# A gated cross-attention block on Trainium2: SyncE's DMA queue in another order

## The reference

```python
x = x + jnp.tanh(g_xattn[0]) * xattn(ctx, ctx, layernorm(x), mask, Wv, bv, Wk, bk, Wq, bq, Wo, bo)
x = x + jnp.tanh(g_ffn[0]) * jnp.tanh(layernorm(x) @ W1 @ W2 @ W3 + bias)
# xattn: energy = where(mask == 0, min, q @ k.T); softmax(energy / sqrt(16)) @ v, then @ Wo + bo
```

## Time and profile before

| | us |
|---|---|
| median of 3 runs (1081.43 to 1085.96) | 1083.36 |
| the profiled execution | 1079.94 |
| its span | 1078.1 |
| TensorE busy | 1023.4 (95%) |
| VectorE busy | 948.6 (88%) |
| ScalarE busy | 828.6 (77%) |
| GpSimd busy | 806.0 (75%) |

### The profile page before, as it was taken

The page is one execution under the profiler, slowest core; times in us unless marked ns, Lnnn a source line. Parts: engine busy times, 40 slices in busy tenths (PEclk is TensorE's granted clock), DMA queues, the critical chain, the costliest instruction groups (busy, mean ns, idle before and its releaser), DMA issues.

```text
span 1078.1 us, 45335 instructions
## 1 busy us (share of the span) xinstructions
PE 1023.4 (95%) x18487; PEld 892.2 (83%) x18487; DVE 948.6 (88%) x1331; ACT 828.6 (77%) x1275; POOL 806.0 (75%) x1184
## 2 busy tenths in 40 slices
PE   5988999999999999999999999999999999999965
PEld 5777888888888888888888888888888888888855
DVE  5778999998899999989999998899998999999866
ACT  4566888888788888878888788788887887878742
POOL 5245878878788887878888877788787887888753
PEclk9999999999999999999999999999999999999998
DMA  5133555555555555555555556555555555555431
GB/s 154 45 104 106 165 147 161 162 155 152 155 153 164 145 171 155 164 149 149 165 154 162 157 145 173 143 161 159 152 164 150 150 163 149 167 152 154 124 124 69
DMA packets 260400, 158.87 MB, mean 147 GB/s; under 512 B 174945, under 2 KB 227170, under 8 KB 260194
## 3 DMA queue, kind: packets, MB, share of 16 engines
q1 hardware_dynamic: 260050, 155.72, 51.4%
q10 hardware_dynamic: 144, 0.26, 0.1%
HBM read 85.92 MB, written 68.94 MB: 144 GB/s over the span
## 4 chain that ended last, share of the span: by engine, by line
PE 55%; DMA 13%; SPq 13%; issue 7%; POOL 6%; DVE 5%; ACT 1%; POOLq 0%; DVEq 0%; ACTq 0%
PE ps_m L507 11%; PE ps_m L500 11%; PE ps_s L636 9%; PE ps_s L615 8%; PE ps_x L647 7%; PE ps_m L574 5%; DMA scratch_y<-yn 5%; SPq L215 3%; DMA scratch_m<-max_T 3%; PE ps_s L621 3%; SPq L303 2%; SPq L292 2%; DMA q_aug<-scratch_m 2%; PE ps_m L494 2%; DMA den_wide<-scratch_r 2%
## 5 line engine op out<-in xcount | busy, mean ns | idle before, releaser
L1021 DVE TENSOR_TENSOR probs<-ps_s,far_T 128x2048 f32<-128x2048 f32 x128 | 293.3, 2291 | 60.0 <-PE ps_s L636 59.8
L1010 DVE TENSOR_REDUCE neg_max<-ps_s 128x16 f32<-128x2048 f32 x128 | 292.5, 2285 | 26.7 <-PE ps_s L621 26.2
L810 ACT ACTIVATE probs<-probs 128x2048 f32<-128x2048 f32 x128 | 245.0, 1914 | 6.2 <-DVE probs L1021 5.9
L785 ACT ACTIVATE q_aug<-ps_m,q_bias,q_scale 128x256 f32<-128x256 f32 x256 | 123.5, 563 | 58.0 <-PE ps_m L500 48.9
L615 PE MATMUL ps_s<-k_aug,q_aug 32*128 32x128 f32 x4096 | 150.6, 283 | 14.2 <-DVE probs L1021 8.1
L636 PE MATMUL ps_s<-q_aug,k_aug 32*128 32x128 f32 x4096 | 152.1, 283 | 8.5 <-DMA q_aug<-scratch_m 5.8
L615 PEld LDWEIGHTS ps_s<-k_aug,q_aug 32*128 32x128 f32 x4096 | 127.9, 186 | 34.9 <-issue 24.3
L636 PEld LDWEIGHTS ps_s<-q_aug,k_aug 32*128 32x128 f32 x4096 | 127.7, 186 | 27.3 <-DMA q_aug<-scratch_m 9.4
L647 PE MATMUL ps_x<-probs,v_ones 128*32 128x128 f32 x4096 | 139.2, 277 | 3.2 <-issue 2.4
L785 ACT ACTIVATE k_aug<-ps_m,k_bias,parity 128x256 f32<-128x256 f32 x256 | 123.5, 563 | 18.8 <-PE ps_m L500 18.8
L647 PEld LDWEIGHTS ps_x<-probs,v_ones 128*32 128x32 f32 x4096 | 104.7, 110 | 32.7 <-issue 32.6
(11 more groups left out here) (123 smaller groups left out, 1725.9 us busy)
## 6 DMA issues: line engine op xcount, KB each, us to landing
scratch_a<-a_den SPq DMA_DIRECT2D x64, 512.0 KB, 3.7
x_in<-in_x SPq DMA_DIRECT2D x64, 256.0 KB, 4.4
a_rows<-scratch_a SPq DMA_DIRECT2D x64, 256.0 KB
den_wide<-scratch_r SPq DMA_DIRECT2D x64, 256.0 KB
out<-y SPq DMA_DIRECT2D x64, 256.0 KB, 4.7
ctx_in<-in_ctx SPq DMA_DIRECT2D x252, 64.0 KB, 2.7
scratch_y<-yn SPq DMA_DIRECT2D x59, 256.0 KB, 4.3
y_blocks<-scratch_y SPq DMA_DIRECT2D x236, 64.0 KB, 2.4
```

The lines of the kernel that those rows point to most:

```text
L785: last = nc.scalar.activation(dst[:, :, 2 * m + a, :], src[:, m * TOK:(m + 1) * TOK].rearrange("p (n q) -> p n q", q=P), ACT.Identity, bia ...
L810: nc.scalar.activation(tile, tile, ACT.Exp).then_inc(probs_ready, 1)
L1010: nc.vector.tensor_reduce(neg_max[:, 0:H].rearrange("p (j c) -> p j c", j=G), ps_s[:], AX.X, ALU.max, negate=True).then_inc(max_ready, 1)
L1021: nc.vector.tensor_tensor(probs[i % 2][:].rearrange("p j s q -> p (j s) q"), ps_s[:].rearrange("p j s q -> p (j s) q"), far_T[:].unsqueeze ...
```

## The change

Only the order in SyncE's queue changes. Block 0 of the ctx load of pair t + 3 is issued between `read_den` and the even `read_max`, ahead of `write_a` and the x load; blocks 1 to 3 stay where the whole load was. The store, which stood at the head of a pass for pair t - 7, is issued behind `read_a` for pair t - 6. The odd `read_max` is issued ahead of `write_y`. The store of pair NP - 7 that followed the loop falls into it.

```diff
-            def load_ctx(p):
+            def load_ctx_blocks(p, blocks):
                 wait(sp, ctx_turned, p - 1)
-                if p == 0:
-                    sp.dma_start(ctx_in[0][:], ctx_v[:, 0]).then_inc(ctx_landed[0], 16)
-                    return
-                for a in range(G):
+                for a in blocks:
...
             for t in range(NP):
-                if is_pair(t - 7):
-                    store(t - 7)
                 if is_pair(t - 5):
                     read_y(t - 5)
                 write_max(2 * t)
                 if is_pair(t - 2):
                     read_den(t - 2)
+                if is_pair(t + 3):
+                    load_ctx_blocks(t + 3, (0,))
                 read_max(2 * t)
                 if is_pair(t - 2):
                     write_a(t - 2)
                 if is_pair(t + 4):
                     load_x(t + 4)
                 if is_pair(t + 3):
-                    load_ctx(t + 3)
+                    load_ctx_blocks(t + 3, (1, 2, 3))
                 write_max(2 * t + 1)
                 if is_pair(t - 2):
                     write_reciprocals(t - 2)
                     read_a(t - 2)
+                if is_pair(t - 6):
+                    store(t - 6)
+                read_max(2 * t + 1)
                 if is_pair(t - 4) and t - 4 <= END:
                     write_y(t - 4)
-                read_max(2 * t + 1)
                 if is_pair(t - 2):
                     read_wide(t - 2)
             y3, y2, y1, last = NP - 4, NP - 3, NP - 2, NP - 1
-            store(NP - 7)
             read_den(y1)
```

More of the change, by code:

```diff
@@ L217, in load_ctx @@
                                  ).then_inc(ctx_landed[p % 2], 16)
+            def load_ctx(p):
+                if p == 0:
+                    sp.dma_start(ctx_in[0][:], ctx_v[:, 0]).then_inc(ctx_landed[0], 16)
+                else:
+                    load_ctx_blocks(p, range(G))
             def load_first():
```

## The result

The changed kernel takes 1107.33 us as the median of 4 runs (1103.88 to 1111.02) beside 1082.39 us of the kernel before on the same chip. The ratio is 1.0222, with an interval of 1.0193 to 1.0251: slower by 2.2%. It is slower, as forecast, but by about twice the 11 us of the likeliest case: it lies inside the stated range of 1076 to 1113 and just above the 1089 to 1106 that was called the likeliest. The profiled execution took 1103.88 us with a span of 1102.1 us, 24.0 us more than the span before.

A forecast was written before the change was run, and what follows sets the result against it. PE sets the pace, with SyncE's loop over write_y's landing next to it. Loop terms -0.3 + 0.65 - 0.2 plus 0.05 for den_wide give +0.20 us a pass, +11.6 us over 58 passes: 1094.5 us, range 1076 to 1113.

The forecast's parts named there:

- The bound: SyncE's loop over write_y's landing, 15.4 to 15.66 us, is at PE's 15.67 us pace; what lengthens it reaches PE.
- the 10.4 us: Time of 58 steady passes above PE's packed pace, claimed as all that any order of SyncE's queue could give back.
- the floor of 1073 us: Lowest time allowed for the rival in which SyncE's loop becomes shorter, priced at 1076 us.
- Step 4: write_y behind store and odd read_max: issued 2.36 us after read_a, landing 5.8 after it; loop +0.65 us, bounds +0.4 and +0.95.
- Step 1: Ctx block ahead of the even read_max: loop gains 0.3 us a pass, bounds 0 and 0.53.
- Step 5: read_y's own issue is stretched less when write_y lands later: -0.2 us a pass, bounds 0 and -0.4.
- Steps 2 and 3: Moved store loses its cover but queues nothing up; odd read_max ahead of write_y gains 0, bounds 0 and -0.8 us.
- Step 6: den_wide lands up to 0.93 us later, through POOL to PE's xn: 0.05 us a pass, bounds 0 and 0.3.
- (c): Store costs its full 0.93 us and den_wide's delay reaches PE: about +0.5 us a pass, 1112 us; chance 0.12.
- (a): SyncE's loop becomes shorter by 0.33 us and up to 10.4 us come back: 1076 us; chance 0.20.
- (b): Nothing changes: the block saves what the landing costs, odd maxima arrive as before: 1083 us, give or take 5; chance 0.25.
- The signs: write_y 2.3 to 2.4 us after read_a, read_y 5.5 to 6.1, no yn wait, passes 16.0 to 16.1, more q_aug waits.

The follow-up runs named there:

- e10: Changed kernel with read_y reading the input x instead of write_y's scratch, so it waits for no landing: 1082.2 us, ratio 0.9986 to the kernel before.
- e2: Kernel before with only the odd read_max moved ahead of write_y: 1088.0 us, ratio 1.0043.
- e4: Kernel before with the ctx block and the odd read_max moved, the store left at the head of the pass: 1084.0 us, ratio 0.9987.
- e5: Changed kernel with the store one place further back, behind write_y: 1091.4 us, ratio 1.0043 to the kernel before.
- e6: Changed kernel with its store writing 16 of 128 token rows, same place, wait and issue: 1083.1 us, ratio 0.9976 to the kernel before.
- e1: Kernel before with only the store moved, behind read_a and ahead of write_y: 1119.5 us, ratio 1.0329.
- e3: Kernel before with only ctx block 0 moved ahead of the even read_max: 1078.9 us, ratio 0.9945.
- e11: Kernel before with read_y reading the input x and not waiting for write_y's landing: 1081.0 us, ratio 0.9961.
- e9: Kernel before with ctx block 0 ahead of the even read_max and read_y put behind the even write of maxima: 1097.4 us, ratio 1.0108.

## Why the prediction was right, and what it mis-sized

**The bound.** Right. SyncE's loop over the landing of `write_y` was at TensorE's pace, and what lengthened it came through. The open loop (e10) shows it. Too much was said of the 10.4 us, though: with the loop open 8.8 to 10.9 us remain, and with the ctx block alone, the best order here, 5.5 (58 passes from 101.22 to 1015.59, a mean of 15.77). No order tried came to the floor of 1073 us; the best median is 1078.3.

**Step 4, the landing.** This term was mis-sized: +0.65 was charged, with +0.95 as the upper bound, and +1.13 was measured (5.13 to 6.26). The ordinary pass is near the forecast, with a median of 6.04 and 37 of 58 passes between 5.5 and 6.1; the other 21 reach up to 7.46 and draw the mean up. The two ends, "the shortest lag after the later issue" and "the old landing plus the store's bytes", were treated as alternatives of which one would hold, and the middle was taken. They add up. The later issue alone puts the landing at 5.54 to 5.66 (e2, e4, e5, e6), which is the lower end, 5.53; the store's bytes come on top with 0.60 (changed against e6), or 0.63 in the time to landing where the store is moved alone (e1). So the landing does mind when `write_y` is issued, by about a third of the delay: in e2 it was issued 1.20 us later and landed 0.41 later. The prediction read from the earlier trace rows that it hardly minds. That holds within the kernel before, for a shorter delay: its 24 passes in which `write_y` came more than 1.1 us after `read_a` landed at 4.95 in the mean, the 27 with less than 0.8 at 5.27. It doesn't hold for the longer delay with the odd read in front. The 0.93 us from the queue's average share was too high for the bytes.

The estimate worked out from the rate in the Trainium skill ("DMA: Bandwidth & Descriptors", "Anatomy of one DMA", a section on DMAs that GpSimd issues) is 0.60 us for 256 KB. The 0.63 of e1 agrees with it for a DMA that SyncE issues; for the 224 KB of e6 the same estimate is 0.53, beside 0.60.

**Step 1, the ctx block.** The mechanism was right and its size of 0.3 us about so: e3 gives 5 to 6 us in time (ratio 0.9945), and its W and L, with the waits for max_T taken out, are some 0.2 shorter. But W and L fall by 0.65 in the changed kernel, more than the bound of 0.53. Two things that the prediction gave no price add to it: the store is gone from the head of the pass (0.27 in e1, 2.21 to 2.04 and 5.23 to 5.13), and the odd read is ahead of `write_y` (0.17 in e2). The three shares are rough, since L holds waits for max_T.

**Step 5, the issue of `read_y`.** Wrong. It was to shrink by 0.2 us as the landing came later; its mean stayed, 2.01 and 2.03, and it is stretched beyond 2.5 us in 10 of 58 passes where it was in 9.

The terms as measured are +1.13 - 0.65 + 0.02 = +0.50, less 0.03 elsewhere, beside a mean pass of TensorE that grew by 0.42 (15.85 to 16.27); the two agree to 0.05. The prediction had +0.20, half of that. Two of its terms were off in opposite directions, the landing by +0.48 and the stretch of step 1 by -0.35, and offset each other in good part, so that the sum came out closer than its terms: this much of it is luck.

**Steps 2 and 3.** Right. The store was covered at the head of the pass: put back there, with the rest of the change in place (e4), it takes the loss away. It waited for nothing of its own in the new place. The odd read gained nothing: its maxima land 5.55 us after `read_a`, before 5.42, in the mean of all passes.

**Step 6, den_wide.** Right in size: TensorE's waits for xn grew by 1.6 us in 58 passes, 0.03 a pass beside the 0.05 charged. It is what takes over as soon as the odd maxima come early (e2, e4, e5).

**Rivals.** (c), 1112 us, had the right size, but by the wrong path: the price was paid at the landing, by the bytes and the later issue together, not through POOL. (a) was true of one part, the ctx block. (b) describes e4.

**The signs.** Of those named, these were seen: the wait for yn gone, the odd read where it was, the even read 2.43 us after its write, more waits for q_aug and for xn. `write_y` was issued 2.3 to 2.4 us after `read_a` in about 40 of 58 passes; in the others an issue behind `read_a` waited or was held back, up to 3.97. The mean pass of 16.27 lies above the 16.0 to 16.1 named.

What stays open: what the remaining long passes are. With the loop open in the changed kernel (e10) 36 of 58 passes are packed, and 11 are above 16 us; four of these hold a wait for xn, 2.7 us together. In the kernel before with its loop open (e11) 8 are above 16 us; four hold waits for q_aug (1.6 us) and two waits for xn (1.2 us). So a part still hangs on when SyncE's reads land; for the rest the profile names hardly any releaser, and no run here was made on it.

## What to carry to other kernels

In a hand-ordered DMA queue, look for the write that is read back and follow the queue around from one landing to the next: its length is the sum of all issues between them, and what is issued during the landing is nearly free, while what is put ahead of the write is paid, here with a third of its issue time and once more with its bytes. Moving the last read or write out of that shadow to fill a gap elsewhere exchanges a covered cost for an open one. Take away one wait, and look at once for what is queued behind the next (e9).

## What the runs showed that was not expected

In this kernel the place of a transfer matters far more than its size: the same 224 KB less were worth 24 to 27 us behind `read_a` and 4 to 6 us at the head of the pass. And the time from issue to landing of the same 256 KB write goes from 3.36 us (e2, with only the small read of maxima issued between `read_a` and it) over 4.15 (before, right behind `read_a`) to 4.78 (e1, behind `read_a` and the store), so it says more of what lies ahead than of the write.
